# State space: the next norm moved into the front and onto ScalarE, all gates but the last on ScalarE and GpSimd, D u on TensorE

## What is computed

```python
xn = layernorm(x)                                # and, for the state space, rmsnorm(xn) * w_norm
xs, res = split(rmsnorm(xn) @ W_in)              # res is "z" below
xs = silu(causal_conv(xs, conv_w, conv_b))       # "u"
A = -exp(A_log);  dt_r, B, C = split(xs @ W_xp)
delta = softplus(dt_r @ W_dt + b_dt)
h_t = h_{t-1} * exp(delta * A) + delta * B * u   # for every channel and state, over time
y = sum_n(C * h) + u * D
attn = (y * silu(res)) @ W_out + rmsnorm(xn)     # residual of the mixer
ffn  = (silu(xn @ gate.T) * (xn @ up.T)) @ down.T
x = x + attn + ffn
```

## Time and profile before

| | |
|---|---|
| profiled execution | 1742.44 us |
| its span, first to last instruction | 1740.7 us |
| median of three runs | 1745.69 us |
| TensorE busy over the span | 1549.9 us (89%) |
| VectorE busy | 1192.6 us (69%) |
| ScalarE busy | 909.2 us (52%) |
| GpSimd busy | 709.4 us (41%) |
| mean granted TensorE clock | 0.967 |

### The profile page before, as it was taken

The page is one execution under the profiler, slowest core; times in us unless marked ns, Lnnn a source line. Parts: engine busy times, 40 slices in busy tenths (PEclk is TensorE's granted clock), DMA queues, the critical chain, the costliest instruction groups (busy, mean ns, idle before and its releaser), DMA issues. The chain is left out here.

```text
span 1740.7 us, 25994 instructions
## 1 busy us (share of the span) xinstructions
PE 1549.9 (89%) x8384; PEld 1213.6 (70%) x8384; DVE 1192.6 (69%) x2524; ACT 909.2 (52%) x1961; POOL 709.4 (41%) x678
## 2 busy tenths in 40 slices
PE   6999869979999888888899898889999897999898
PEld 4767658877777788644445455577887786888787
DVE  5888847667778678789979993336666444666633
ACT  5555436765665556564445443235655444665543
POOL 5999843215222233177919773112221332212222
PEclk9999979999999999999999998899999998999999
DMA  3222122101112122050014000011111112111111
GB/s 126 76 67 69 37 90 91 65 22 56 49 48 88 51 71 85 28 195 1 1 51 171 0 1 7 7 47 34 49 45 58 55 55 64 44 48 36 71 55 49
DMA packets 34331, 98.35 MB, mean 57 GB/s; under 512 B 6388, under 2 KB 11256, under 8 KB 32072
## 3 DMA queue, kind: packets, MB, share of 16 engines
q1 hardware_dynamic: 33064, 90.95, 15.5%
q0 software_dynamic: 1184, 6.37, 1.1%
HBM read 96.12 MB, written 1.18 MB: 56 GB/s over the span
## 5 line engine op out<-in xcount | busy, mean ns | idle before, releaser
L881 POOL TENSOR_TENSOR head_low<-head,head_high 128x512 fp32r<-128x512 f32 x64 | 81.8, 1278 | 459.1 <-ACT head_high L871 458.3
L1780 POOL TENSOR_TENSOR experts_low<-experts,experts_high 128x1536 fp32r<-128x1536 f32 (+1 forms) x64 | 144.7, 2264 | 282.1 <-ACT experts_high L1726 160.1
L1233 ACT ACTIVATE probs<-banks,neg_max 128x512 f32<-128x512 f32 (+3 forms) x256 | 131.4, 526 | 150.7 <-DVE neg_max L1143 150.7
L2292 POOL TENSOR_TENSOR rings<-du,bc_rows 128x512 f32<-128x512 f32 x126 | 160.4, 1285 | 105.5 <-DMA bc_rows<-bc_rows 75.5
L2028 PE MATMUL banks<-rings,ident 128*128 128x512 f32 x256 | 135.1, 630 | 35.0 <-DVE rings L2244 34.5
L2215 DVE TENSOR_TENSOR_SCAN banks<-banks,rings 128x512 f32<-128x512 f32 x128 | 155.8, 1219 | 3.3 <-POOL rings L2292 1.6
L2130 ACT ACTIVATE banks<-delta,A 128x512 f32<-128x512 f32 x128 | 88.6, 692 | 116.5 <-DVE rings L2244 116.4
L219 PE MATMUL banks<-experts_high,xnT_high 128*128 128x384 f32 (+1 forms) x384 | 139.5, 363 | 6.4 <-POOL experts_low L1780 6.4
L1477 DVE SCALAR_TENSOR_TENSOR hidden<-banks,weight,act_out 128x96 f32<-128x96 f32 (+1 forms) x192 | 62.7, 368 | 115.1 <-ACT act_out L1445 114.6
L1445 ACT ACTIVATE act_out<-banks 128x256 f32<-128x256 f32 (+2 forms) x112 | 47.5, 424 | 175.1 <-PE banks L219 174.8
L219 PE MATMUL banks<-experts_low,xnT_high 128*128 128x384 f32 (+1 forms) x384 | 137.5, 358 | 0.0
(11 more groups left out here) (278 smaller groups left out, 4713.1 us busy)
## 6 DMA issues: line engine op xcount, KB each, us to landing
head<-in_heads SPq DMA_DIRECT2D x64, 384.0 KB, 3.0
experts<-in_experts SPq DMA_DIRECT2D x16, 1152.0 KB, 5.2
bc_rows<-bc_rows SPq DMA_DIRECT2D x30, 512.0 KB, 5.9
experts<-in_experts SPq DMA_DIRECT2D x16, 768.0 KB, 4.2
values<-in_values SPq DMA_DIRECT2D x32, 256.0 KB, 3.2
coef<-in_spline_coef POOLq DMA_DIRECT2D x8, 768.0 KB, 4.6
idx<-in_lut_idx SPq DMA_DIRECT2D x16, 134.0 KB, 2.1
x<-in_x SPq DMA_DIRECT2D x2, 512.0 KB, 4.4
```

Of the source, the lines that this page charges most:

```text
L1233: last = nc.scalar.activation(prob_tile(i), score_tile(i), ACT.Exp, bias=neg_max[:, i:i + 1], scale=QK_SCALE, accum_out=row_sum[:, i:i + 1])
L1780: nc.gpsimd.tensor_tensor(parts[gpar][1][:, columns], raw[gpar][:, columns], parts[gpar][0][:, columns].bitcast(FP32), ALU.subtract)\
L2292: nc.gpsimd.tensor_tensor(inflow[:, step % INFLOWS], du[:, c], B_of(n), ALU.mult)\
```

## The change

In both state-space stages:

- Norm: statistics run on VectorE at the start of the front, the root on ScalarE after `take_x(0)` with the root table loaded ahead, and the inverse roots after the copy of B and C (`roots_early`). The scaling is four ScalarE activations at step 26 (`scale_scalar`), the rescaling by the rms four more at step 42 (`scale_again_scalar`).
- MLP: for the first 15 items ScalarE also copies `up` out of PSUM and adds one to the tanh a step later; GpSimd multiplies half gate with up (one step later again) and the result with the raised tanh. Item 15 stays as it was.
- z: scaled by 0.5 as it is taken, tanh, plus one on ScalarE, one GpSimd product; groups 0 and 1 at steps 17 to 24 now.
- D u: GpSimd makes diagonal matrices of D in the front, TensorE adds diag(D) u to y by one matmul for each group; `take_y` is gone and `gate_y` reads y from PSUM.
- The joins come at steps 37 and 43. VectorE makes inflows 0 and 1, GpSimd from 2 on.

```diff
+    def roots_early(self, dve):
+        dve.wait_ge(self.rooted.sem, self.rooted.at(1))
+        reciprocal_root(nc, chain, self.roots)
+        chain.all(nc.vector.scalar_tensor_tensor(m.rs[:, 4, 0], m.mv[:, :, 0], -1.0, m.rs[:, 3, 0],
+                                                 ALU.mult, ALU.mult))
+        if self.with_rms:
+            chain.all(nc.vector.tensor_copy(self.rms[:], m.rs[:, 3, 1]))
+        dve.sem_inc(self.inverted.sem, 1)
+    def scale_scalar(self, act):
+        act.wait_ge(self.inverted.sem, self.inverted.at(1))
+        act.wait_ge(*self.xn_free)
+        for t in range(NT):
+            m.nc.scalar.activation(m.xn[:, t], self.x[:, t], ACT.Identity, scale=m.rs[:, 3, 0, t:t + 1],
+                                   bias=m.rs[:, 4, 0, t:t + 1]).then_inc(self.normed.sem, 1)
+    def scale_again_scalar(self, act):
+        act.wait_ge(self.turned.sem, self.turned.at(KD))
+        act.wait_ge(self.added.sem, self.added.at(1))
+        for t in range(NT):
+            xn = self.m.xn[:, t]
+            self.m.nc.scalar.activation(xn, xn, ACT.Copy, scale=self.rms[:, t:t + 1]).then_inc(self.scaled.sem, 1)
...
+    on_pool = lambda i: i < ITEMS - 1
+    RAISE_AT = {step + 3: i for step, i in GATE_AT.items() if on_pool(i)}
+    TIMES_UP_AT = {step + 4: i for step, i in GATE_AT.items() if on_pool(i)}
-    Z_BEND = {35: 0, 41: 1, 47: 2, 53: 3}
-    Z_TIMES, Z_PLUS = {38: 0, 44: 1, 50: 2, 56: 3}, {39: 0, 45: 1, 51: 2, 57: 3}
-    Y_GATE = {46: 0, 51: 1}
-    JOIN_AT = {48: 0, 55: 1}
+    Z_BEND, Z_RAISE = {17: 0, 21: 1, 39: 2, 45: 3}, {18: 0, 22: 1, 40: 2, 46: 3}
+    Z_TIMES = {20: 0, 24: 1, 42: 2, 48: 3}
+    SKIP_AT = {10: 0, 13: 1, 35: 2, 39: 3}
+    JOIN_AT = {37: 0, 43: 1}
-    NORM_VECTOR = {20: norm.stats, 26: norm.scale}
-    NORM_ROOT = 24
+    NORM_SCALE = 26
-    if norm.with_xm:
-        NORM_VECTOR[40] = norm.scale_again
+    NORM_AGAIN = 42 if norm.with_xm else None
...
+        def skip_u(c):
+            if c == 0:
+                pe.wait_ge(skip_ready.sem, skip_ready.at(1))
+            nc.tensor.matmul(y_psum(c), skip[:, c], u[:, c], start=False, stop=False)
+            if step in SKIP_AT:
+                skip_u(SKIP_AT[step])
...
+        nc.scalar.preload_act_table_set("sqrt_and_others")
         act.wait_ge(vec_loaded.sem, vec_loaded.at(16))
         take_x(0)
+        norm.root(act)
         take_x(1)
         silu_u(0)
...
                 nc.scalar.activation(hidden[item % 2][:], gate_psum, ACT.Tanh, scale=0.5).then_inc(gate_bent.sem, 1)
+                if on_pool(item):
+                    nc.scalar.activation(up[:], up_psum, ACT.Copy).then_inc(up_taken.sem, 1)
+            if step in RAISE_AT:
+                item = RAISE_AT[step]
+                act.wait_ge(gate_bent.sem, gate_bent.at(item + 1))
+                bend = hidden[item % 2][:]
+                nc.scalar.activation(bend, bend, ACT.Identity, bias=1.0).then_inc(gate_raised.sem, 1)
...
+            if step in Z_RAISE:
+                act.wait_ge(z_bent.sem, z_bent.at(Z_RAISE[step] + 1))
+                nc.scalar.activation(bent[:], bent[:], ACT.Identity, bias=1.0).then_inc(z_raised.sem, 1)
+            if step == NORM_SCALE:
+                norm.scale_scalar(act)
+            if step == NORM_AGAIN:
+                norm.scale_again_scalar(act)
...
     def vector(dve):
         chain = Chain(dve, dve_chain)
+        norm.stats(dve)
...
+        norm.roots_early(dve)
...
-        nc.vector.tensor_tensor(inflow[:, 1], du[:, 1], B_of(0), ALU.mult).then_inc(own_inflow.sem, 1)
+        for c in range(2):
+            dve.wait_ge(du_ready.sem, du_ready.at(c + 1))
+            nc.vector.tensor_tensor(inflow[:, c], du[:, c], B_of(0), ALU.mult).then_inc(own_inflow.sem, 1)
...
-        def take_y(c):
-            nc.vector.scalar_tensor_tensor(u[:, c], u[:, c], vec[:, c, 6:7], y_psum(c), ALU.mult, ALU.add)\
-              .then_inc(y_taken.sem, 1)
         def gate_y(c):
             dve.wait_ge(summed.sem, summed.at(2 * NS * (c // 2 + 1) - 1 + c % 2 + PRODUCTS))
             dve.wait_ge(z_gated.sem, z_gated.at(c + 1))
+            nc.vector.tensor_tensor(u[:, c], y_psum(c), silu_z[:, c], ALU.mult).then_inc(gated_y.sem, 1)
...
             if c >= 2 and n == 0:
-                take_y(c - 2)
+                gate_y(c - 2)
...
-            if step in GATE_AT:
+            if step in GATE_AT and not on_pool(GATE_AT[step]):
-            if step in Y_GATE:
-                gate_y(Y_GATE[step])
-            if step in NORM_VECTOR:
-                NORM_VECTOR[step](dve)
...
     def gpsimd(pool):
+        def times_up(i):
+            pool.wait_ge(up_taken.sem, up_taken.at(i + 1))
+            nc.gpsimd.tensor_tensor(half_gate[:], half_gate[:], up[:], ALU.mult).then_inc(gate_step.sem, 1)
         def finish(i):
+            if on_pool(i):
+                pool.wait_ge(gate_step.sem, gate_step.at(i + 1))
+                pool.wait_ge(gate_raised.sem, gate_raised.at(i + 1))
...
             bend = hidden[i % 2][:]
             nc.gpsimd.tensor_tensor(bend, bend, half_gate[:], ALU.mult).then_inc(hidden_ready.sem, 1)
+        pool.wait_ge(bc_written.sem, bc_written.at(16))
+        nc.gpsimd.tensor_tensor(skip, m.ident[:].unsqueeze(1).broadcast_to([P, KC, P]),
+                                vec[:, :, 6:7].broadcast_to([P, KC, P]), ALU.mult).then_inc(skip_ready.sem, 1)
...
+            if step in TIMES_UP_AT:
+                times_up(TIMES_UP_AT[step])
...
             if step in Z_TIMES:
-                nc.gpsimd.tensor_tensor(bent[:], bent[:], silu_z[:, z], ALU.mult).then_inc(z_step.sem, 1)
-            if step in Z_PLUS:
-                nc.gpsimd.tensor_tensor(silu_z[:, z], silu_z[:, z], bent[:], ALU.add).then_inc(z_gated.sem, 1)
+                nc.gpsimd.tensor_tensor(silu_z[:, z], silu_z[:, z], bent[:], ALU.mult).then_inc(z_gated.sem, 1)
```

More of the change, by code:

```diff
@@ L2158, in scalar @@
                     act.wait_ge(z_gated.sem, z_gated.at(z))
-                nc.scalar.activation(bent[:], silu_z[:, z], ACT.Tanh, scale=0.5).then_inc(z_bent.sem, 1)
-            if step == NORM_ROOT:
-                norm.root(act)
+                nc.scalar.activation(bent[:], silu_z[:, z], ACT.Tanh).then_inc(z_bent.sem, 1)
+            if step in Z_RAISE:
[3 more added lines that the diff above has]
+                norm.scale_scalar(act)
             if step in NORM_STORE:
                 norm.store(act, NORM_STORE[step])
+            if step == NORM_AGAIN:
+                norm.scale_again_scalar(act)
             if step in XM_STORE:
@@ L2251, in vector @@
                 nc.vector.scalar_tensor_tensor(bend, bend, 1.0, up_psum, ALU.add, ALU.mult).then_inc(up_taken.sem, 1)
-            if step in Y_GATE:
-                gate_y(Y_GATE[step])
-            if step in NORM_VECTOR:
-                NORM_VECTOR[step](dve)
             if step in NORM_LOW:
                 norm.low(dve, NORM_LOW[step])
-        for c in (2, 3):
-            take_y(c)
-            gate_y(c)
+        gate_y(2)
+        gate_y(3)
         dve_chain.close(chain.n)
     def gpsimd(pool):
+        def times_up(i):
+            pool.wait_ge(up_taken.sem, up_taken.at(i + 1))
+            nc.gpsimd.tensor_tensor(half_gate[:], half_gate[:], up[:], ALU.mult).then_inc(gate_step.sem, 1)
         def finish(i):
-            pool.wait_ge(half_taken.sem, half_taken.at(i + 1))
-            pool.wait_ge(up_taken.sem, up_taken.at(i + 1))
+            if on_pool(i):
+                pool.wait_ge(gate_step.sem, gate_step.at(i + 1))
+                pool.wait_ge(gate_raised.sem, gate_raised.at(i + 1))
+            else:
+                pool.wait_ge(half_taken.sem, half_taken.at(i + 1))
+                pool.wait_ge(up_taken.sem, up_taken.at(i + 1))
             bend = hidden[i % 2][:]
             nc.gpsimd.tensor_tensor(bend, bend, half_gate[:], ALU.mult).then_inc(hidden_ready.sem, 1)
+        pool.wait_ge(bc_written.sem, bc_written.at(16))
+        nc.gpsimd.tensor_tensor(skip, m.ident[:].unsqueeze(1).broadcast_to([P, KC, P]),
+                                vec[:, :, 6:7].broadcast_to([P, KC, P]), ALU.mult).then_inc(skip_ready.sem, 1)
         for step in range(STEPS):
             c, n = channel_of(step), state_of(step)
-            if step == 1:
+            if step < 2:
                 continue
@@ L2277, in gpsimd @@
                 pool.wait_ge(du_ready.sem, du_ready.at(c + 1))
-            if step == 0:
-                pool.wait_ge(first_row.sem, first_row.at(16))
-            elif step < 2 * NS and step % 2 == 0:
+            if step < 2 * NS and step % 2 == 0:
                 pool.wait_ge(rows_loaded[n % 4].sem, rows_loaded[n % 4].at(16 * (n // 4 + 1)))
             if step == 2:
-                pool.wait_ge(own_inflow.sem, own_inflow.at(1))
-            if step == 3:
-                pool.wait_ge(du_ready.sem, du_ready.at(2))
+                pool.wait_ge(own_inflow.sem, own_inflow.at(2))
             if step >= INFLOWS:
@@ L2310, in gpsimd @@
                 z = Z_TIMES[step]
```

(5 more changed lines are left out.)

42 lines of the change are left out of this document (21 added, 21 removed).

## The result

The changed kernel takes 1727.26 us (median of four runs, 1725.26 to 1732.32) against 1745.18 us (four runs, 1740.93 to 1746.28) of the kernel before: a ratio of 0.9902 with a 95% interval of 0.9884 to 0.9921, or 18 us less. The forecast was 1720, its range 1710 to 1733. Direction and range held; of the 24 us in the forecast's sum, 18 came. A second series of six runs gave 0.9895 (0.9874 to 0.9916).

A forecast was written before the change was run, and what follows sets the result against it. VectorE was taken to set the loop's end. 32.0 - 2 x 0.3 (front) - 2 x 2.5 (GpSimd) - 1.1 (input add) - 1.3 (TensorE) = 24.0 us gained; forecast 1720 us, own range 1714 to 1726, with rivals 1710 to 1733.

The forecast's parts named there:

- What leaves VectorE: 32 us: Gates, gate waits, norm work and y gates leave VectorE's queue: 18.0 us in batch 0, 14.0 in batch 1.
- Front: 0.3 us lost a batch: Before the first scan, moved norm work and table loads hide; GpSimd's D product costs +0.3 us a batch (-0.3 to +1.2).
- the rule of shared interfaces: GpSimd contends with VectorE instructions of two SBUF inputs; scan and product, with one PSUM operand, are left alone.
- GpSimd: 2.2 us at the end of its lead: Inflows 11 to 25: GpSimd's deficit of 6.5 us less its lead of 4.3 makes VectorE wait 2.2 us a batch.
- the 0.3: Added to GpSimd's wait: ScalarE's half_gate copy waits for GpSimd's previous finish, delaying the decays queued behind; 0.3 us.
- The input add: 1.1 us: Steps 33 to 48 of batch 0: GpSimd's add of the input costs about 1.1 us more; batch 1 has none.
- TensorE: 0.3 and 1.0 us: Crowded steps 32 to 47: TensorE late, holding up ScalarE; 0.3 us in batch 0, 1.0 in batch 1, bounds 0 and 2.5.
- The signs: If right: loops some 14 and 10 us shorter, ring waits at scans 20 to 28, one table load, TensorE over 94% busy.
- Nothing late: Rival, 0.12: GpSimd's lead is larger than counted, so all 32 us come; about 1712 us.
- ring through three engines: Rival, 0.20: ScalarE, GpSimd and TensorE wait on one another, some 0.5 us an item, 13 us for 26; about 1730.
- Identity operations: Rival, 0.07: ScalarE's new Identity operations bring table loads beside exp, adding 59 us to ScalarE; with waits about 1742 us.
- The clock: Rival, 0.04: TensorE's clock drops to 1.2 GHz, each item there loses 5.15 us; from six items slower, 1752 or more.

The follow-up runs named there:

- half_gate2: The changed kernel with two buffers each for half gate and up instead of one; stages 150.73 and 150.24 us, against 150.22 and 151.80.
- norm_only: The kernel before with the norm's part of the change alone; 1726.85 us (median of four), ratio 0.9877.
- scale_spread: The changed kernel with ScalarE's four norm scalings at steps 12, 15, 24 and 27, not all at 26; stages 149.34 and 150.70 us.

## Why the prediction was right, and where it was off

*What leaves VectorE: 32 us.* Right. Batch 0's loop fell by 12.05 us and has new waits of 4.73 + 0.95 + 0.92 (block; scans 42, 43; scan 50): 18.65, forecast 18.0 (scan 2's new 1.5 us and the 1.5 us at scan 5 that went cancel). Batch 1: 7.80 + 4.71 + 0.37 + 2.40 less 0.71 won at scan 2 is 14.6, forecast 14.0.

*Front: 0.3 us lost a batch.* Wrong sign, small: the first scan comes 24.52 us after the join instead of 25.00 and 24.94. The collision with GpSimd that the prediction set against the new inflow 0 (+0.6 us) was worth more than that. One VectorE operation in front of batch 0's first scan took 1.64 us while GpSimd made its first inflow, and takes 0.69 now (before, after):

```profile
747.14 1.64 DVE L2197 TENSOR_TENSOR du<-delta,u 128x512 f32<-128x512 f32 x1
...
749.72 0.69 DVE L2255 TENSOR_TENSOR du<-delta,u 128x512 f32<-128x512 f32 x1
```

VectorE's statistics, root and `roots_early` hid as worked out, the silu table load between two takes cost nothing (first tap operations 8.99 us for twelve, as in the earlier trace rows). The D product ran at 745.90 for 1.05 us, mostly in the wait before `delta+du` (746.74), which took 0.75 instead of 0.69 us: 0.06, not 1.2. The two overlapped for only 0.2 us, so this place is no test of the rule of shared interfaces that the prediction cites from the Trainium skill (GPSIMD Engine Reference, section 8, Key points); the operation of 1.64 us above, with two SBUF inputs, agrees with it. That scan and product, with one operand in PSUM, are left alone was borne out: with GpSimd 92% busy over the loop products took 675 ns on average, 672 before.

*GpSimd: 2.2 us at the end of its lead, plus 0.3 for ScalarE.* The first number was nearly right: the waits put down to GpSimd's rings are 0.20 + 1.33 + 0.84 = 2.37 us in each batch, at scans 21 to 25, where the sum had them; with the small delays of 0.1 to 0.2 us around them they cost 3.1, as half_gate2 shows, where only they are left. **The step that failed is the 0.3.** ScalarE's share was 1.6 us, by name (0.54 + 1.05) and by what half_gate2 took off the block. A half-gate copy that waits 2.57 us was priced as a small tax on the lead, and the four scalings at 0.27 us of pitch each, 1.06 in all; they took 2.07. I had taken the pitch of copies with constant scale for an operation with a scale and a bias read per partition. ScalarE: Activation LUTs, section "What ACT_TABLE_LOAD costs", in the Trainium skill has it: about 93 ns more for each such operand. An estimate by its figures (186 + 0.833 x 256 + 2 x 93) is 585 ns for one; the trace has 601 in the changed kernel and 585 in norm_only, against 376 for the tanh. half_gate2 and scale_spread show the two causes: without the late copy no wait at 26 or 27, without the scalings at step 26 none at 27.

*The input add: 1.1 us* (its own terms, 30.1 - 27.5 - 1.3, give 1.3). Not there in the changed kernel (no wait at scan 34), but latent: 1.14 us came in half_gate2 and 0.71 in scale_spread, when ScalarE no longer gave GpSimd time. The term was about right as a sum of work and wrong as an addition: what VectorE had lost to ScalarE at scans 26 and 27, GpSimd did not cost it again at 34.

*TensorE: 0.3 and 1.0 us, bounds 0 to 2.5.* Measured 1.87 in batch 0 (scans 42, 43 and 50, all gone when its work was moved) and 2.8 in batch 1, just past the bound. The size was low in both batches, and the path was wrong. I had it hold up ScalarE's tanh. It held up the norm's transposes instead: in batch 0 ScalarE's copies of them stand before the decays, and in batch 1 VectorE waits for such a copy directly. That operation of VectorE (`low`) had been written off as "stays".

*The sum.* Forecast 24.0 us, stages 20.96. The block costs 4.4 more than taken, TensorE 1.8 more in batch 1 and, with the add, 0.5 in batch 0; against that 1.2 more left VectorE, the front came out 1.5 better and scan 2 of batch 1 gave 0.7: 24.0 - 6.7 + 3.4 = 20.7. The last 0.2 is the tail behind scan 63, 8.20 us instead of 8.31 and 8.30. That misses of 6.7 and 3.4 us have opposite signs is luck: scan 2's 0.7 is scatter, and the front's gain had been put down as a loss. The intervals of the two series are 14 to 20 and 15 to 22 us, so that the stages' 21 and the medians' 18 us agree only loosely; the scatter of the rest of the program is large enough for the difference.

*The signs.* Waits for GpSimd's rings at scans 20 to 28 came, a little over 2 us a batch, with one table load in batch 0's loop and 3.2 us of idle put down to ScalarE's decay, under the 5 us named for the ring. The loops shrank by 12 and 8 us instead of 14 and 10, and TensorE was 93% busy over batch 0's loop, not over 94%.

*Rivals.* "Nothing late" is out. The "ring through three engines" was real, but stood at three items of batch 0 (the half-gate copies at 785.52, 791.79 and 799.31), not at 13, and cost 1.6 us a batch, not 6.5: it bites only where GpSimd's lead is gone. No table loads came with the Identity operations (one load of 1.28 us in ScalarE's loop). The clock rose to 0.99 over the loop.

What the forecast did not ask, and should have: what each part is worth alone. By its own sums the gates give 9.9 us and cost GpSimd one more product of 0.68 us every third step; with all gates on VectorE some four of the nine products between inflows 11 and 25 go, the deficit of 6.5 us falls to 6.5 - 4 x 0.68 = 3.8, and the lead of 4.3 us covers it, so that the 5.0 us of waits in the block fall away. That sum was there to be made: 9.9 less 5.0 leaves 5 us of gain at most. Measured is none.

## What to carry to other kernels

When the bound engine is relieved, work it out part by part: here the norm's part, which moved work into idle time before the loop and onto ScalarE, brought 17 us of 21, and the gates' part, which moved work onto GpSimd at 81% of the loop as well as onto ScalarE, brought nothing. Once three engines have equal work in a loop, price a new operation by the lead that it eats where it stands, and sum that over a stretch, not over the loop. A single buffer between an in-order engine and a nearly full one costs nothing until the lead is gone, and then adds to the wait: 3.1 us of block with two buffers, 4.7 with one. A second buffer for two small tiles, three of fifteen items moved back, the four scalings spread out and TensorE's D u and joins placed elsewhere together brought 7 us in the stages (302.0 to 294.9) and 9 in the medians.

## What the runs showed of the hardware

- ScalarE on 128x256: 376 ns for a tanh from PSUM with constant scale, 498 with one per-partition operand, 601 with two (groups of ScalarE in the changed kernel's loop). The pitch of four in a row was 0.40 us with one such operand and 0.49 with two.
- A GpSimd product of a broadcast identity and a broadcast column, 128x512, took 1.05 us, against 1.27 for two full operands.
- A VectorE product with both inputs in SBUF, 128x512, took 1.64 us beside a GpSimd product and 0.69 otherwise, while VectorE's products of a PSUM and an SBUF operand took 675 ns on average with GpSimd 92% busy.
- TensorE's granted clock over the eight microseconds behind the first join was 0.77 to 0.81 in three of twelve profiles and 1.00 in the others; that cost the stage 1.7 us.
- VectorE's waits in the block repeated to 0.02 us between batches and executions of the changed kernel, while code that nobody changed varied by 7.7 us (1416.6 to 1424.3) from one execution to the next. For changes of a few microseconds the stretch in the profile tells more than the total.
